# Attention block on one core: two steps per phase of values, five score banks ahead, outputs transposed by VectorE from their bank

## The reference, cut to what matters

```python
x = x + layernorm(attention(layernorm(x)))     # 16 heads of 16 channels, softmax over 1024 keys, then w_o
x = x + layernorm(ffn(layernorm(x)))           # r = sigmoid(xr W_r), k = relu(xk W_k)^2, out = r * (k W_v)
# xr and xk mix each token with the one before it: mu * x + (1 - mu) * x_prev
```

## Time and profile before

| | |
|---|---|
| median of 3 runs | 1271.68 us (1270.45 to 1273.1) |
| the profiled execution | 1271.37 us, span 1269.6 us |
| TensorE matmuls busy | 1250.9 us, 99% of the span |
| TensorE weight loads | 601.9 us, 47% |
| ScalarE | 1065.5 us, 84% |
| VectorE | 781.7 us, 62% |
| GpSimd | 269.1 us, 21% |
| granted TensorE clock | 0.999 of full |

### The profile page before, as it was taken

One profiled execution on the slowest core, in us unless ns is written; L12 is line 12 of the kernel. 1 busy time (PEld: TensorE's weight loads), 2 busy tenths in 40 slices (PEclk: granted clock), 3 DMA queues, 4 the chain that ended last, 5 costly groups with the idle time before them and its releaser, 6 DMA issues.

```text
span 1269.6 us, 25462 instructions
## 1 busy us (share of the span) xinstructions
PE 1250.9 (99%) x10604; PEld 601.9 (47%) x10604; DVE 781.7 (62%) x1738; ACT 1065.5 (84%) x1155; POOL 269.1 (21%) x351
## 2 busy tenths in 40 slices
PE   8999999999999999999999999999999999999997
PEld 5544454444444445454544444444444444534345
DVE  7644746658465773847557584666747466364647
ACT  4788888888888888888888888888888888898872
POOL 2000212222211322222121221222221122222121
PEclk9999999999999999999999999999999999999999
DMA  4455564317712194124733166321751129400000
GB/s 154 128 133 170 103 128 79 92 51 132 119 51 84 52 181 85 52 66 105 147 68 112 43 112 130 76 84 51 149 118 45 42 68 177 91 1 18 18 16 19
DMA packets 61796, 112.69 MB, mean 89 GB/s; under 512 B 6512, under 2 KB 31344, under 8 KB 61616
## 3 DMA queue, kind: packets, MB, share of 16 engines
q1 hardware_dynamic: 61360, 109.60, 38.3%
q10 hardware_dynamic: 288, 1.05, 0.3%
HBM read 68.42 MB, written 41.94 MB: 87 GB/s over the span
## 4 chain that ended last, share of the span: by engine, by line
PE 94%; DVE 2%; ACT 2%; DMA 1%; issue 0%; POOL 0%; SPq 0%; DVEq 0%
PE O L480 39%; PE S L470 27%; PE M L425 24%; PE M L373 3%; PE M L401 2%; ACT PT L538 2%; DMA xA<-x_dram 1%; DVE sth L728 0%; DVE A L736 0%; DVE QS L690 0%; ACT QS L566 0%; DVE A L988 0%; DVE xB L858 0%; POOL rsh L1089 0%; DVE st L676 0%
## 5 line engine op out<-in xcount | busy, mean ns | idle before, releaser
L538 ACT ACTIVATE PT<-S 128x1024 f32<-128x1024 f32 x1024 | 1003.3, 1026 | 158.4 <-PE S L470 157.7
L480 PE MATMUL O<-PT,V 128*17 128x512 f32 x4096 | 538.9, 598 | 0.1
L470 PE MATMUL S<-QS,KS 50*128 50x512 f32 x2048 | 465.5, 450 | 3.7 <-ACT PT L538 3.7
L470 PEld LDWEIGHTS S<-QS,KS 50*128 50x128 f32 x2048 | 211.1, 184 | 453.1 <-ACT PT L538 376.4
L480 PEld LDWEIGHTS O<-PT,V 128*17 128x17 f32 x4096 | 67.9, 95 | 140.3 <-issue 137.6
L1087 POOL TENSOR_SCALAR veh<-mvh 128x2 f32<-128x2 f32 x96 | 22.3, 232 | 489.2 <-DVE mvh L731 487.5
L988 DVE SCALAR_TENSOR_TENSOR A<-Z,M 128x512 f32<-128x512 f32 x30 | 20.4, 682 | 159.4 <-PE M L425 159.4
L425 PE MATMUL M<-xnT,WH 64*128 64x512 f32 x496 | 108.0, 393 | 0.0
L425 PE MATMUL M<-WH,xnT 64*128 64x256 f32 x480 | 79.6, 278 | 0.0
L425 PE MATMUL M<-WH,C 64*128 64x256 f32 x480 | 78.6, 278 | 0.8 <-issue 0.8
L425 PE MATMUL M<-WH,cT 64*128 64x256 f32 x480 | 78.7, 278 | 0.0
(11 more groups left out here) (152 smaller groups left out, 1648.5 us busy)
## 6 DMA issues: line engine op xcount, KB each, us to landing
scr<-p SPq DMA_DIRECT2D x124, 256.0 KB
QS<-scr SPq DMA_DIRECT2D x56, 256.0 KB, 6.5
KS<-scr SPq DMA_DIRECT2D x56, 256.0 KB, 10.5
QS<-scr SPq DMA_DIRECT2D x70, 128.0 KB, 5.7
KS<-scr SPq DMA_DIRECT2D x68, 128.0 KB, 8.0
xA<-x_dram SPq DMA_DIRECT2D x16, 512.0 KB, 7.1
xB<-x_dram SPq DMA_DIRECT2D x16, 512.0 KB, 7.3
out_dram<-xB SPq DMA_DIRECT2D x15, 512.0 KB, 3.1
```

Of the source, the lines that this page charges most:

```text
L470: ins = e.matmul(PS[pair][:, a, :], KS[qd][rows, pair, kt * 128:kt * 128 + 128], QS[qd][rows, pair, hf * 512:hf * 512 + 512], start=True, ...
L480: ins = e.matmul(PO[32 * j:32 * j + 17, :], V[b % 2][:, kt, 4 * qd + j, :], PT[i % 2][:, j, :], start=(kt == 0), stop=(kt == 7))
L538: e.activation(PT[i % 2][:, 2 * pair:2 * pair + 2, :], PS[pair][:, :, :], ACT.Exp, scale=SCALE) \
```

## The change

From step 12 (`PAIRED`) on TensorE works in periods of two steps. In a period it runs the three scores that are late (`LATE`: heads 0, 2 and 3 of step i+1), the projections of both steps in portions between scores, both turns if there are any, then five scores ahead (`AHEAD`: head 1 of step i+3 and heads 0 to 3 of step i+2), and last the values of both steps without a break. Five banks belong to scores (`HEAD_BANKS`); of the remaining ones PO keeps one and two rotate among the pieces. The first half of a turn uses the bank of head 1. Scores are issued head by head, each with its own semaphore update. ScalarE takes heads 0, 2+3 and, for the following step, 0+1, 2+3, and the single head 1 of the step after that; PT has three buffers instead of two.

VectorE's transpose reads PO itself from the second quad on, and the next quad's values wait for that transpose; the second stage of a quad comes first among the rests. A y piece is copied to A first, which frees its bank, and statistics and norm read A; this copy waits for A to be free (`a_free`, `("added", u - 1, 1)`). The first half of a T turn is copied to On first and split from there one step later. In FIRST and LAST some pieces move by one step, so that turns begin at even steps. The buffers of the correction get smaller, to make room for PT.

The core of the diff:

```diff
+PAIRED = 12
+LATE = ((1, 0), (1, 2), (1, 3))
+AHEAD = ((1, 1), (0, 0), (0, 1), (0, 2), (0, 3))
+HEAD_BANKS = ((0, 1, 2, 3), (0, 4, 2, 3))
...
-FIRST = {2: "V2", 3: "K01", 4: "V3", 5: "Q10", 6: "K10", 7: "K11", 8: "Q01", 9: "Q11", 11: "T0", 15: "Q00", 17: "K00",
-         19: "T1", 23: "Q01", 25: "K01"}
+FIRST = {2: "V2", 3: "K01", 4: "V3", 5: "Q10", 6: "K10", 7: "K11", 8: "Q01", 9: "Q11", 12: "T0", 14: "Q00", 16: "K00",
+         18: "T1", 22: "Q01", 24: "K01"}
 NEXT_TO_LAST = {2: "V3", 4: "y0", 6: "y1", 14: "z", 20: "k0", 22: "k1", 24: "r0", 26: "r1", 28: "v0", 30: "v1"}
-LAST = {4: "y0", 6: "y1", 13: "z", 17: "k0", 19: "k1", 21: "r0", 23: "r1", 25: "v0", 27: "v1"}
+LAST = {4: "y0", 6: "y1", 12: "z", 16: "k0", 18: "k1", 20: "r0", 22: "r1", 24: "v0", 26: "v1"}
...
-STAGES = {"y": 3, "v": 2}
+STAGES = {"y": 3, "v": 2, "T": 2}
...
     if word == "quad":
         return 3 if n % 2 else 2
+    if word in ("T01", "T11"):
+        return 1
     if word == "z1":
         return 5 if n < UNITS - 2 else 1
...
-        then = [i + 1] if i < 8 else [j for j in range(at[-1] + 1, i + 12) if j < STEPS and not turns[j]][:2]
+        then = [i + 1] if i < 8 else [i + 2] if i == 9 else [j for j in range(at[-1] + 1, i + 12) if j < STEPS and not turns[j]][:2]
...
-        waiting += [(piece, 1) for piece, _ in end + rest if stages_of(piece) > 1]
+        waiting += [(piece, 1) for piece, _ in end if stages_of(piece) > 1]
+        quads = [(piece, 1) for piece, _ in rest]
         for piece, stage in rested[:2]:
             rest.append((piece, stage))
             if stage + 1 < stages_of(piece):
                 waiting.append((piece, stage + 1))
-        waiting[:0] = rested[2:]
+        waiting[:0] = quads + rested[2:]
...
+def late_heads(i):
+
+    return [(i + n, j) for n, j in (LATE if i > PAIRED else ((1, 0), (1, 1), (1, 2), (1, 3)))]
+
+
+def ahead_heads(i):
+    return [(i + 2 + n, j) for n, j in AHEAD] if i + 2 < STEPS else []
...
+    fifth, free = free[0], free[1:]
+    at = {0: ("exp", PAIRED, 0), 1: ("exp", PAIRED, 1), 2: ("exp", PAIRED, 2), 3: ("exp", PAIRED, 3), 4: fifth[1]}
+    number = [0, 1, 2, 3, fifth[0]]
...
+    def take_for(i, j):
+        k = HEAD_BANKS[i % 2][j]
+        of[i, j], freed[i, j], at[k] = number[k], at[k], ("exp", i, j)
+
+    for i in range(PAIRED, STEPS, 2):
+        for user in late_heads(i):
+            take_for(*user)
         if TURNS[i]:
-            take(TURNS[i])
-            leave(TURNS[i], 0)
-        for piece, stage in RESTS[i]:
-            leave(piece, stage)
+            of[TURNS[i]], freed[TURNS[i]], at[1] = number[1], at[1], ("bank", TURNS[i])
+            take(TURNS[i + 1], free)
+            free.append(left(TURNS[i + 1]))
+        elif HALVES[i][0]:
+            take(HALVES[i][0][0], free)
+        for user in ahead_heads(i):
+            take_for(*user)
+        if not TURNS[i]:
+            free += [left(piece) for piece, _ in ENDS[i + 1]]
...
-        PT = [sb(f"PT{i}", [128, 4, 512]) for i in range(2)]
+        PT = [sb(f"PT{i}", [128, 4, 512]) for i in range(3)]
...
-        C16 = sb("C16", [16, 2, 128])
-        R16 = sb("R16", [16, 2, 128])
+        top_hi, top_lo = sb("top_hi", [16, 128]), mask[0:16, :]
...
+        PB = ctx.enter_context(nc.psum_tensor("M", [128, 7, 512], F32))
         PO = ctx.enter_context(nc.psum_tensor("O", [128, 512], F32))
-        PM = [ctx.enter_context(nc.psum_tensor(f"M{i}", [128, 512], F32)) for i in range(3)]
+        PS = [PB[:, 2 * i:2 * i + 2, :] for i in range(2)]
+        PM = [PB[:, k, :] for k in range(7)]
...
+            left, took = [[], []], [0.0, 0.0]
+
+            def gather(i):
+
                 for row, half_ in enumerate(HALVES[i]):
                     if half_:
                         piece, part = half_
                         every = list(moving_of(*piece)(rows_of(row)))
                         mine = every if part == 2 else every[part * len(every) // 2:(part + 1) * len(every) // 2]
-                        left[row] = [(piece, part != 1 and k == 0, part and k + 1 == len(mine), len(every), *one)
-                                     for k, one in enumerate(mine)]
+                        left[row] += [(piece, part != 1 and k == 0, part and k + 1 == len(mine), len(every), *one)
+                                      for k, one in enumerate(mine)]
+
+            def halves(enough=99.0):
+
                 while left[0] or left[1]:
                     row = 1 if not left[0] or left[1] and took[1] < took[0] else 0
+                    if took[row] > enough:
+                        break
...
-            def scores(i, pair):
-                if i == STEPS:
-                    return
+            def score(i, j):
                 b, qd, hf, kt = heads[i]
-                if kt == 0 and pair == 0:
-                    maxima(b, qd, hf, i)
+                pair, a = j // 2, j % 2
                 p.wait_ge(("rows", 0), ("rows", 1))
                 if b == qd == hf == 0:
                     p.wait_ge(("flag",), in_quad(b, qd, 0, hf)[pair], in_quad(b, qd, 1, kt // 4)[pair])
                 else:
                     p.wait_ge(*in_quad(b, qd, 0, hf), *in_quad(b, qd, 1, kt // 4))
-                if i:
-                    p.wait_ge(("exp", i - 1, pair))
-                for a in range(2):
-                    rows = slice(64 * a, 64 * a + ROWS)
-                    ins = e.matmul(PS[pair][:, a, :], KS[qd][rows, pair, kt * 128:kt * 128 + 128],
-                                   QS[qd][rows, pair, hf * 512:hf * 512 + 512], start=True, stop=True)
-                ins.then_inc(*up(pe_wrote, ("scores", i, pair)))
+                if freed[i, j]:
+                    p.wait_ge(freed[i, j])
+                rows = slice(64 * a, 64 * a + ROWS)
+                e.matmul(PM[bank[i, j]], KS[qd][rows, pair, kt * 128:kt * 128 + 128],
+                         QS[qd][rows, pair, hf * 512:hf * 512 + 512], start=True, stop=True) \
+                    .then_inc(*up(pe_wrote, ("scores", i, j)))
+                took[a] += .216
...
             def values(i):
                 b, qd, hf, kt = heads[i]
-                p.wait_ge(("exp", i, 0), ("exp", i, 1), ("V", b, kt // 2))
+                p.wait_ge(*[("exp", i, j) for j in range(4)], ("V", b, kt // 2))
                 if kt == 0:
                     p.wait_ge(("PO", i // 8 - 1))
                 for j in range(4):
-                    ins = e.matmul(PO[32 * j:32 * j + 17, :], V[b % 2][:, kt, 4 * qd + j, :], PT[i % 2][:, j, :],
+                    ins = e.matmul(PO[32 * j:32 * j + 17, :], V[b % 2][:, kt, 4 * qd + j, :], PT[i % 3][:, j, :],
                                    start=(kt == 0), stop=(kt == 7))
...
+            def period(i):
+
+                late, ahead = late_heads(i), ahead_heads(i)
+                took[:] = 0.0, 0.0
+                for n in range(2):
+                    gather(i + n)
+                for one in late[:-2]:
+                    score(*one)
+                halves(.1)
+                for one in late[-2:]:
+                    score(*one)
+                for n in range(2):
+                    if TURNS[i + n]:
+                        turn(TURNS[i + n])
+                halves(.55)
+                if ahead:
+                    if heads[i + 2][3] == 0:
+                        maxima(*heads[i + 2][:3], i + 2)
+                    score(*ahead[0])
+                    halves(1.25)
+                    for one in ahead[1:3]:
+                        score(*one)
+                halves()
+                for one in ahead[3:5]:
+                    score(*one)
+                values(i)
+                values(i + 1)
...
+                period(i)
...
+            def exponentials(i, *numbers):
+
+                if i >= STEPS:
                     return
-                p.wait_ge(("scores", i, pair))
-                if i >= 2:
-                    p.wait_ge(("values", i - 2))
-                e.activation(PT[i % 2][:, 2 * pair:2 * pair + 2, :], PS[pair][:, :, :], ACT.Exp, scale=SCALE) \
-                    .then_inc(*up(act_wrote, ("exp", i, pair)))
+                j, k, at = numbers[0], numbers[-1], bank[i, numbers[0]]
+                p.wait_ge(("scores", i, j), ("scores", i, k))
+                if i >= 3:
+                    p.wait_ge(("values", i - 3))
+                e.activation(PT[i % 3][:, j:k + 1, :], PB[:, at:at + len(numbers), :], ACT.Exp, scale=SCALE) \
+                    .then_inc(*up(act_wrote, *[("exp", i, n) for n in numbers]))
...
+                exponentials(i + 1, 0)
+                if i == PAIRED:
+                    exponentials(i + 1, 1)
+                exponentials(i + 1, 2, 3)
+                exponentials(i + 2, 0, 1)
+                for (word, n), stage in ENDS[i + 1]:
                     if word[0] == "r":
                         sigmoids(n, int(word[1]))
-                exponentials(i + 1, 1)
-                if i % 8 == 7 and i < STEPS - 1:
-                    outputs(i // 8)
```

(35 more changed lines are left out.)

113 lines of the change are left out of this document (60 added, 53 removed).

## The result

The changed kernel takes 1310.22 us (median of 4 runs, 1309.05 to 1313.45) against 1271.66 (4 runs, 1270.45 to 1273.1): a ratio of 1.0307, 95% interval 1.0285 to 1.0328. The forecast was 1262, in a range that ended at 1284: wrong in sign, and off by 48 us.

A forecast was written before the change was run, and what follows sets the result against it. TensorE was taken as the bound, busy 99%. Gains of 5.0 (even) and 5.2 us (odd units) met stalls of 5.2 and 4.9; with units 0, 14 and 15, -9 in all: 1271.4 - 9 = 1262 us, range 1236 to 1284.

The forecast's parts named there:

- Part 1: TensorE, one phase of values per two steps: removes one visit, 0.33 us, giving 4.39 us per full period.
- the choice of 0 for ordering: TensorE's row groups: no idle time from matmul order, with 0.11 us per period kept as the bound.
- rival C: TensorE matmuls start in order: 0.11 us in each of 147 periods, 16 us in all, 1278 us; chance 0.07.
- Part 4: Two rotating banks instead of three: TensorE waits for VectorE, stalls of 5.2 us per even unit, 4.9 per odd.
- The waits of the projections for VectorE's p and V rows: Sign: new waits of projections' weight loads or scores for VectorE's p, V and Z/T rows, some 60 us, largest before k0.
- rival D: TensorE's clock falls in new idle stretches before k0: up to 1310 us, a third more likely, 1278; chance 0.06.
- the odd units' stalls: TensorE waiting for VectorE in odd units: 1.5 after y, 2.9 after z, 0.5 small, together 4.9 us.
- rival B: VectorE's stretch between z and k0 takes 1 us or more longer by cast collisions: 1275, two 1288 us; chance 0.17.
- small ones: Score 1 behind the turned tile's copy at T0 and z, 0.2 us each, and next input's statistics: 0.5 a unit.
- Part 3: VectorE transposes from the output bank: cover 1.8 us, cost 0, but VectorE idles in the period after a turn.
- Turn periods: Periods with turns on TensorE: about 4.3 us against 4.5 per pair before, a gain of 0.25 us.
- Weight loads of the values waiting for "issue": Sign on TensorE: these waits, 506 before the change, would come about half as often.

The follow-up runs named there:

- the filled version: Changed kernel with two (odd units) or three (even units) needless matmuls put into TensorE's wait before k0: 1288.82 us, ratio 1.0135.
- the third experiment: Kernel before, unpaired, with VectorE transposing outputs from their bank, ScalarE's copy gone but for the first, quads first in VectorE's order: 1306.05 us, ratio 1.0285.
- the fastest version: Changed kernel with mixing before the quad after z1, the norm late, and z1's last two mixing stages and y1's norm behind bank-freeing pieces: 1215.33 us.
- second experiment: Changed kernel with the first mixing stage after z1 put ahead of the quad's turn in VectorE's order: 1268.57 us, ratio 0.9979.

## Why the prediction was wrong, step by step

**Right.** Part 1: the full period (4.39 forecast, 4.38 measured), the visit of 1.84, and the choice of 0 for ordering; rival C fell. By the rule of the Trainium skill's page "TensorE: Matmul & The Clock Gate", Part 3, section "The mechanism", the period would have been 4.50; the trace has 4.38. Part 4's places: each wait it named is there (after y, at k0 for the Q or V piece's bank), and in even units its sizes: 1.2 us for the y wait (5.58 against 4.38) where 1.5 was forecast, 3.40 idle for 3.2. The waits of the projections for VectorE's p and V rows come to 53.5 us, where some 60 with the Z and T rows were forecast. Even units at full clock, as the filled version shows them, take 75.53 us against a forecast of 75.0.

**Failed first: the clock, a term that the sum put at 0.** Part 4 put a pause of 3 us before k0 into 13 units, and the sum charged each pause once, with its own length. That the clock falls in it stood in rival D alone, with a chance of 0.06 and "a third of that" held more likely, with no row for the third. The earlier trace rows bear on it, if less closely than it may seem: 0.78 over 5.6 us is, between the levels of 1.0 and 0.5, 2.5 us at half clock, so the fall came 3.1 us into that stretch; but the trace has TensorE's last matmul end at 1262.33, so the engine had then been idle for 4.8 us. That a pause of 3 us is enough no row of before shows, and none shows that it isn't: the longest pause in mid-span was 1.5 us (1235.78 to 1237.24). With both open, 0.06 was too little and a third had no ground. Measured: some 25 us in units 1 to 13, and 2.5 in unit 0, whose period of 6.90 has no wait in it and TensorE busy throughout, at a mean clock of 0.61: 28 us of the 48. That D's upper end, 1310, is what came is luck: it priced the clock at 48 us, and the other 20 are stalls that D did not have.

**Failed second: the odd units' stalls, 4.9 us forecast.** At full clock an odd unit takes 77.15, not 75.0. The y wait came to 1.4 (5.79) and k0's to 3.0 (7.34), as forecast, but ahead of k0's stood one of 1.5 in period 9, for a copy of V that frees a bank, which the sum didn't hold apart (its 2.9 was for all between z and k0), and the norm's at period 2 came to 0.85 where it was one of the "small ones". Behind it is rival B's mechanism, in odd units only: VectorE's stretch between z and k0 is 13.32 us in unit 7 where 12.30 was taken, and 1.0 of it is the norm beside GpSimd's addition (2.35 for 1.37); in even units it did not grow (12.52 for 12.61). Units 1, 3, 5, 7, 9, 11 and 13 came out 1.25, 2.1, 2.2, 2.15, 2.1, 2.1 and -0.55 over their 75.0, 11 us. Unit 13, which has no next input to norm beside it, has neither wait. Moving the norm out of the way took both waits away in the others too, 3.1 us a unit in six units, with the clock at half for as long as before.

**Failed third: the first long period of unit 0.** Its 7.12 us hold waits of 1.14 (for VectorE's p rows) and 0.59 (for the copy to On) around the turns, and its end runs at half clock; the sum had 4.3. That is some 2.5 us over the 4.60 of other turn periods.

Of the 48 us, then, 28 are the clock, 11 the odd units' stalls, 3 the even units' half a microsecond each, 2.5 unit 0's waits, and 2 unit 14, which went from 72.4 to 70.8 us where a gain of 3.5 was forecast. The rest was not taken apart.

**Part 3, "cover 1.8 us, cost 0",** was right for the bank: no wait of the values for the transpose (L892) is among the changed kernel's waits of 1.5 us and more. Its last sentence named the danger, the idle VectorE after a turn. The idle time itself was in part 4's 3.2 us, since there VectorE's stretch starts with period 8; what was not asked is what the order is worth, 41.7 us with the clock's part in it: the costliest edit of the change is its smallest.

**Smaller misses.** Turn periods are 4.60, not 4.3 and 0.2 for a stall; the terms that the prediction lists for one add up to 4.35, which against 4.5 is a gain of 0.15 and not of 0.25. Weight loads of the values waiting for "issue" were to be half as many and are 727 instead of 506: so that row doesn't count visits, as the prediction took it to; what it does count was not followed further. VectorE's busy share did not rise (62%), since the span grew too.

**Open.** How the 8 us of the third experiment's last unit divide between the bank, the order and the clock; why k0's period with fillers is 8.05 rather than 4.38 and the 3.2 forecast. In the fastest version, unit 0's two periods (7.74 and 5.51), the turn periods of 4.60 and the even units' y period (4.99) are left; no version was run against them.

## What to carry to other kernels

A saving on the bottleneck engine is only had if the engine that frees its buffers keeps to the new deadlines, and an average load of 62% says nothing about that: write down, for each buffer, when it is wanted and which instructions stand ahead of the one that frees it, and put bank-freeing work before work that nobody waits for. Here changes of order alone (the mixing ahead of the quad, the norm later in the unit, the pieces that free a bank ahead of z1's mixing and y1's norm), with the same 1782 instructions on VectorE, moved the time from 1310 to 1215 us. An idle stretch of TensorE was charged twice here, once as idle time and once as slow matmuls behind it, so a forecast with pauses of 2 to 3 us has to carry the second charge in its main case.

## What was not expected of the hardware

- The granted clock halved around an idle stretch of 2.17 us as well as of 3.40, and in unit 0 around two of 1.14 and 0.59; at pauses of 2.13 to 2.18 us it fell in 7 cases and stayed up in 5 (second experiment, and the norm moved late with its order). It stayed down for 3.41 or 6.83 us, with TensorE at work for most of it (starts 0.43 us apart instead of 0.24). The Trainium skill's page "TensorE: Matmul & The Clock Gate", Part 1, section "What's actually happening", gives two states that one will see, 1.2 and 2.4 GHz; the trace agrees, its records show 0.5 and 1.0.
- VectorE, working between SBUF tiles beside one GpSimd addition of 1.3 us, loses 0.9 to 1.0 us (0.43 to 1.38, 0.75 to 1.66, four short ones 1.37 to 2.35), and an addition that starts inside such an operation grows too, 1.29 to 1.7; beside copies out of a bank neither side grew. With 62% of VectorE and 21% of GpSimd busy this fell on the stretch between z and k0 in both units whose timelines were read (6 and 7).
- Pairing with four score banks takes 4.83 us per period, more than the two steps it replaces (4.72): TensorE and ScalarE then take turns in waiting for each other.
